# A decoder layer with routed experts: the last 48 rows of each expert's down weights split into high and low parts and stacked in 128 rows, and row numbers computed one block earlier

## The chip, the cores and the metric

The kernel runs on one core of one Trainium2 chip. The time is the device time of one execution in microseconds (us). The median of three runs of the kernel before is 344.32 us (343.75 to 344.35).

The engines in this text: PE is TensorE (matrix products), PEld its loading of stationary operands, DVE is VectorE, ACT is ScalarE, POOL is GpSimd, SP is SyncE, which here does nothing but wait, load registers and start DMAs.

## The reference

One decoder layer on 8 sequences of 128 rows of 256 values: self-attention with a sliding window, cross-attention, and a feed-forward part with 16 experts, of which each row takes four, plus a shared expert. The part that the change touches:

```
topk_w, topk_ids = top_k(softmax(x @ gate_w.T), 4)
for w13_e, w2_e, e in experts:            # 16 of them; w13_e is 352 x 256, w2_e is 256 x 176
    coef = sum(where(topk_ids == e, topk_w, 0))
    g, u = split(x @ w13_e.T)             # 176 and 176 columns
    acc += ((silu(g) * u) @ w2_e.T) * coef
out = shared(x) + acc
```

All inputs and outputs are float32.

## The kernel before

**Front (up to about 195 us).** Both attentions run as a software pipeline over the 8 sequences; `iteration(t)` is written out on each engine for the first and last values of t and is a loop for the middle ones. Beside it POOL splits the shared expert's weights (`split_shared`, a copy to the reduced type float32r and a subtraction that leaves the low part), and SP clears 17 MB of DRAM (`x_slots`). Routing follows: DVE computes the place of each of a row's four picks (`route_slots`), and POOL scatters the rows with 32 indirect DMAs (`scatter`, L538) into `x_slots`, where each expert's rows lie together. DVE and ACT split the experts' up weights into `w13_h` and `w13_l`; POOL does the last three low parts itself (L606).

**Block stage (about 195 to 314 us).** The rows of `x_slots` are worked off in 47 blocks of 128 rows, each for one expert. For a block n:

- SP loads the expert's down weights into `w2` (`load_down`, L432 and L433) and the block's rows into `xb` (`load_rows`, L424 to L426). Each takes a register load of the expert or row number from `table`, then a DMA. Both tiles have 4 buffers. `load_rows` waits until block n-4 has been transposed (`xbt_psum`) and its row numbers are made (`ids_ready`); `load_down` waits until the products of block n-4 are done (`yb_psum`). SP's order is `load_rows(n + 5)`, `load_down(n + 3)`, then the next n.
- PE transposes `xb` (`turn_block`, L1772), ACT copies it out as float32r (`take_rows_t`, L812), DVE subtracts for the low part (`low_rows_t`, L1270). PE makes the up product in six float32r matmuls (`block_up` through `three`, L1524: high by high, high by low, low by high, two halves each). ACT takes silu (`block_gate`, L820), DVE multiplies (`block_hidden`, L1278) into `hb`, padded from 176 to 256 columns with zeros. PE transposes it (`turn_hidden`, L1792), ACT copies it out (`take_hidden_t`, L827), and PE multiplies by `w2` in two float32 matmuls (`block_down`, L1802), each of which the trace shows as two records. DVE scales the result (`take_block`, L1285), and POOL writes it with an indirect DMA (`place_rows`, L613) to the places in `ids`, which DVE computes in three small steps (`block_ids`, L1290 to L1294).

PE's order in an iteration n is written out: `turn_block(n + 2)`, `block_up(n + 1)`, `turn_hidden(n)`, `block_down(n - 1)`. DVE's is `low_rows_t(n + 2)`, `block_hidden(n + 1)`, `block_ids(n + 1)`, `take_block(n - 1)`. ACT's is `take_rows_t(n + 2)`, `block_gate(n + 1)`, `take_hidden_t(n)`.

**End (314 us on).** PE finishes the second half of the shared expert, while SP gathers the experts' results into `yg`; DVE adds all up, and SP stores the output.

Of the kernel before, what the change touches and what calls it, by code (L numbers as in the profile page):

```python
# [7 lines left out]
F32 = mybir.dt.float32  # L8
F32R = mybir.dt.float32r
# [27 lines left out]
GU = 2 * HE  # L37
REGION = B * T
# [20 lines left out]
def decoder_layer(nc, x_in, ctx_in, keys_in, wqkv_in, bqkv_in, wo_in, bo_in, rope_in, masks_in, gate_in,  # L59
                  w13_in, w2_in, shared_in, ident_in, iota_in, tri_in, upto_in, table_in, picks_in, dump_in, packs_in, out):  # L60
    ctx = ExitStack()
    with ctx:
# [24 lines left out]
        ident_b = place("ident_b", [128, 128], BF16)  # L87
        masks = place("masks", [128, 2, TILES, 128], BF16)
        zero_b = place("zero_b", [128, 2 * XW], BF16)
# [91 lines left out]
        wo = place("wo", [128, KC, D])  # L181
        rope = place("rope", [128, 2, ROT])
# [4 lines left out]
        qkv = place("qkv", [128, QKV])  # L187
        turned = place("turned", [128, ROT])
# [32 lines left out]
        w2 = place("w2", [128, RB, KC, D])  # L221
        xbt_h = place("xbt_h", [128, 2, KC, 128], F32R)
        xbt_l = place("xbt_l", [128, 2, KC, 128], F32R)
        hb = place("hb", [128, 2, D])
        hbt = place("hbt", [128, 2, KC, 128])
        cursor[0] = max(cursor[0], after_cross)
        sb("slab", [128, (cursor[0] - base) // 4])
        x_slots = nc.dram_tensor("x_slots", [EMPTY + 128, XW], F32)
        y_picks = nc.dram_tensor("y_picks", [YROW, D], F32)
# [133 lines left out]
        hbt_ready = sem("hbt_ready")  # L363
        yb_psum = sem("yb_psum")
# [14 lines left out]
        def _(sp):  # L379
# [24 lines left out]
            for c in range(1, B):  # L404
                load_keys(c)
                if 2 <= c <= SC:
                    sp.wait_ge(swl_ready, c - 1)
                    sp.dma_start(sw_raw[:, :], shared_in[c - 1]).then_inc(sw_loaded, 16)
                if c == 1:
# [18 lines left out]
            def load_down(n):  # L428

                if n >= RB:  # L430
# [3 lines left out]
                             w2_in[bass.ds(e, 1)].rearrange("e p k d -> p (e k d)")).then_inc(w2_loaded[n % RB], 16)  # L434

            sp.wait_ge(x3_ready, B)
            sp.wait_ge(table_ready, 3)
            for n in range(RB - 1):
                load_down(n)
# [25 lines left out]
        def _(pool):  # L465
# [107 lines left out]
            for t in (B - 2, B - 1):  # L573
                iteration(t)
# [46 lines left out]
        def _(act):  # L621
# [193 lines left out]
            def block_gate(n):  # L815

                act.wait_ge(gu_psum, n + 1)
                if n >= 2:
                    act.wait_ge(hb_ready, n - 1)
                act.activation(sg[:, n % 2, :], ps_gu[n % 2][:, 0:HE], ACT.Silu).then_inc(sg_ready, 1)  # L820

            def take_hidden_t(n):

                act.wait_ge(hbt_psum, n + 1)
                if n >= 2:
                    act.wait_ge(yb_psum, n - 1)
                act.activation(hbt[:, n % 2, :, :], ps_ht[n % 2][:, 0:KC * 128].rearrange("p (k n) -> p k n", k=KC),  # L827
                               ACT.Copy).then_inc(hbt_ready, 1)
# [4 lines left out]
            for n in range(NBLK):  # L833
# [4 lines left out]
                take_hidden_t(n)  # L838

# [1079 lines left out]
```

## Time and profile before

| | us |
|---|---|
| median of three runs | 344.32 |
| the profiled execution | 343.41 |
| its span, first to last instruction | 341.6 |
| PE busy | 308.8 (90%) |
| DVE busy | 241.5 (71%) |
| ACT busy | 186.7 (55%) |
| POOL busy | 146.6 (43%) |

The profiled execution is one run; its span is 1.81 us shorter than its own time, and its own time is 0.91 us under the median. Times in the trace count from the start of the span. "Busy" is an average over stages with different limits; for a stage the waits and the queue of SP say more. In rows of the trace a merged row shows its start, its duration, the engine, the line, what is written from what, and how many instructions; the bracket at the end is the idle time before it and what ended it. SPq is SP's instruction queue; its DMA rows show when a DMA is issued, not when it lands.

### The profile page before, as it was taken

How to read it: one execution, taken by the hardware profiler on the slowest of the kernel's cores; microseconds unless marked ns; L12 is line 12 of the kernel's file. 1: busy time of each engine (PE TensorE's matmuls, PEld its weight loads, DVE VectorE, ACT ScalarE, POOL GpSimd, SP SyncE). 2: the span in 40 equal slices, each digit the busy share in tenths (PEclk: the TensorE clock that was granted, in tenths of full speed). 3: DMA queues.
4: the chain of work that ended last, by engine and by line, in shares of the span. 5: the costliest groups of instructions: out<-in, count | busy, mean ns of one | idle time of the engine just before them, and what ended most of it. 6: DMA issues, size and time to landing. Idle time of an engine off the chain costs nothing.

```text
span 341.6 us, 8504 instructions
## 1 busy us (share of the span) xinstructions
PE 308.8 (90%) x2606; PEld 238.2 (70%) x2608; DVE 241.5 (71%) x720; ACT 186.7 (55%) x538; POOL 146.6 (43%) x179
## 2 busy tenths in 40 slices
PE   6897899999999997879997789998999989999983
PEld 2354576667667764658775578787978979888862
DVE  2357788988888799563887856576766666765396
ACT  1052889888898977473697333343434434342231
POOL 3584133544544413487578253333434434345000
PEclk9999999999999998996999989999999999999998
DMA  7997197989899941023122526777777777774681
GB/s 210 302 389 307 25 310 179 302 248 291 242 264 266 239 141 33 16 98 113 54 94 96 157 66 187 214 218 233 209 230 210 220 224 213 229 220 149 249 319 61
DMA packets 44153, 66.84 MB, mean 196 GB/s; under 512 B 5347, under 2 KB 31988, under 8 KB 43604
## 3 DMA queue, kind: packets, MB, share of 16 engines
q1 hardware_dynamic: 39476, 54.91, 55.0%
q0 software_dynamic: 3792, 10.56, 8.1%
q10 hardware_dynamic: 848, 0.92, 1.2%
q8 instruction: 19, 0.31, 0.4%
q14 instruction: 18, 0.15, 0.2%
HBM read 37.07 MB, written 29.30 MB: 194 GB/s over the span
## 4 chain that ended last, share of the span: by engine, by line
PE 53%; DVE 9%; DMA 8%; issue 8%; SPq 8%; POOL 7%; ACT 6%; DVEq 0%; ACTq 0%; POOLq 0%
PE bank L1524 16%; PE bank L1802 6%; DMA xb<-x_slots 6%; POOL x_slots L538 5%; PE bank L1441 5%; PE bank L1450 5%; ACT probs L650 4%; PE bank L1394 3%; PE bank L1459 3%; SPq L425 3%; PE bank L1772 2%; SPq L432 2%; PE bank L1483 2%; PE bank L1792 2%; PE bank L1562 2%
## 5 line engine op out<-in xcount | busy, mean ns | idle before, releaser
L613 POOL DMA_INDIRECT y_picks<-yb,ids x47 | 45.1, 960 | 70.0 <-DVE yb L1285 69.4
L650 ACT ACTIVATE probs<-bank,neg_max 128x128 f32<-128x128 f32 x256 | 70.7, 399 | 2.7 <-DVE neg_max L903 2.5
L1802 PE MATMUL bank<-w,hbt 128*128 128x256 f32 x188 | 48.3, 380 | 0.0
L903 DVE TENSOR_REDUCE neg_max<-bank 128x4 f32<-128x512 f32 x64 | 42.1, 683 | 5.8 <-PE bank L1441 5.7
L1450 PE MATMUL bank<-ident,probs 128*128 128x128 f32 x256 | 36.9, 281 | 2.6 <-ACT probs L650 2.6
L812 ACT ACTIVATE xbt_h<-bank 128x256 fp32r<-128x256 f32 x47 | 18.0, 384 | 38.5 <-PE bank L1772 38.4
L538 POOL DMA_INDIRECT x_slots<-x,slots x32 | 34.5, 1080 | 9.3 <-issue 8.9
L1450 PEld LDWEIGHTS bank<-ident,probs 128*128 128x128 f32 x256 | 29.1, 143 | 12.4 <-ACT probs L650 10.3
L1802 PEld LDWEIGHTS bank<-w,hbt 128*128 128x128 f32 x188 | 32.1, 190 | 2.5
L1278 DVE TENSOR_TENSOR hb<-sg,bank 128x176 f32<-128x176 f32 x47 | 15.9, 337 | 24.0 <-ACT sg L820 24.0
L820 ACT ACTIVATE sg<-bank 128x176 f32<-128x176 f32 x47 | 14.9, 317 | 30.2 <-PE bank L1524 30.2
L1270 DVE TENSOR_TENSOR xbt_l<-bank,xbt_h 128x256 fp32r<-128x256 f32 x47 | 19.9, 424 | 11.6 <-ACT xbt_h L812 8.6
L1524 PE MATMUL bank<-w_h,xbt_h 128*128 x94 | 27.5, 373 | 0.0
L1772 PE MATMUL bank<-ident,xb 128*128 128x128 f32 x94 | 18.9, 284 | 6.8 <-DMA xb<-x_slots 6.5
L1285 DVE TENSOR_SCALAR yb<-bank,offset 128x256 f32<-128x256 f32 x47 | 22.7, 483 | 2.0 <-PE bank L1802 2.0
L1524 PE MATMUL bank<-w_h,xbt_l 128*128 x94 | 23.4, 331 | 0.0
L1524 PE MATMUL bank<-w_l,xbt_h 128*128 x94 | 23.3, 330 | 0.0
L1772 PEld LDWEIGHTS bank<-ident,xb 128*128 128x128 f32 x94 | 12.0, 143 | 15.2 <-DMA xb<-x_slots 9.2
L509 POOL TENSOR_TENSOR rstd<-ve,expo 128x1 f32<-128x1 f32 x16 | 9.1, 570 | 26.0 <-DVE ve L953 26.0
L485 POOL TENSOR_TENSOR turned<-qkv,rope 128x320 f32<-128x320 f32 x8 | 6.9, 863 | 29.5 <-DVE qkv L884 29.5
L827 ACT ACTIVATE hbt<-bank 128x256 f32<-128x256 f32 x47 | 18.0, 383 | 1.8 <-PE bank L1792 1.8
L1792 PE MATMUL bank<-ident,hb 128*128 128x128 f32 x94 | 18.0, 273 | 0.7 <-issue 0.5
(175 smaller groups left out, 677.6 us busy)
## 6 DMA issues: line engine op xcount, KB each, us to landing
x_slots<-zero_b SPq DMA_DIRECT2D x16, 1072.0 KB, 10.9
w<-w_in_dram SPq DMA_DIRECT2D x47, 256.0 KB, 3.1
xb<-x_slots SPq DMA_DIRECT2D x47, 134.0 KB
w<-w_in_dram SPq DMA_DIRECT2D x4, 1408.0 KB, 12.6
yg<-y_picks SPq DMA_DIRECT2D x8, 512.0 KB, 7.0
sw_raw<-shared_in_dram SPq DMA_DIRECT2D x6, 384.0 KB, 3.4
ktc<-keys_in_dram SPq DMA_DIRECT2D x8, 256.0 KB, 3.2
ctx_sb<-ctx_in_dram SPq DMA_DIRECT2D x1, 1024.0 KB, 12.6
```

Source lines behind the costliest of these rows:

```text
L538: pool.indirect_dma_start(x_slots[:, :], bass.IndirectOffsetOnAxis(slots[:, TOPK * b + k:TOPK * b + k + 1], 0), x[:, b, :], None).then_inc ...
L613: pool.indirect_dma_start(y_picks[:, :], bass.IndirectOffsetOnAxis(ids[:, n:n + 1], 0), yb[:, n % RB, :], None).then_inc(yb_placed[n % RB] ...
L650: ins = act.activation(probs[:, g, j, :], ps_s[kind][g][:, 128 * j:128 * j + 128], ACT.Exp, bias=neg_max[:, kind, g, j:j + 1])
L812: act.activation(xbt_h[:, n % 2, :, :], ps_xt[n % 2][:, 0:KC * 128].rearrange("p (k n) -> p k n", k=KC), ACT.Copy).then_inc(xbt_high, 1)
L903: dve.tensor_reduce(neg_max[:, kind, g, :], ps_s[kind][g].rearrange("p (j n) -> p j n", j=BLK), AX.X, ALU.max, negate=True).then_inc(max_r ...
L1270: dve.tensor_tensor(xbt_l[:, n % 2, :, :], ps_xt[n % 2][:, 0:KC * 128].rearrange("p (k n) -> p k n", k=KC), xbt_h[:, n % 2, :, :].bitcast( ...
L1285: dve.tensor_scalar(yb[:, n % RB, :], ps_yb[n % 2][:, 0:D], offset[:, n % RB, 1:2], None, ALU.mult).then_inc(yb_ready, 1)
L1450: ins = pe.transpose(ps_s[kind][g][:, 128 * j:128 * j + 128], probs[:, g, j, :], ident[:, :])
L1524: ins = pe.matmul(outs, w, m, start=first and i == 0, stop=last and i == len(todo) - 1, skip_group_check=not (first and last))
L1772: ins = pe.transpose(ps_xt[n % 2][:, 128 * k:128 * k + 128], xb[:, n % RB, 128 * k:128 * k + 128], ident[:, :])
L1792: ins = pe.transpose(ps_ht[n % 2][:, 128 * k:128 * k + 128], hb[:, n % 2, 128 * k:128 * k + 128], ident[:, :])
L1802: ins = pe.matmul(ps_yb[n % 2][:, 0:D], hbt[:, n % 2, k, :], w2[:, n % RB, k, :], start=k == 0, stop=k == KC - 1)
```

## The change

**Down weights.** An expert's down weights have 176 rows. Before, they stand in DRAM as 256 rows with 80 of zeros. Now the first 128 rows stay float32 (`w2_in`), and the last 48 come as an input of their own (`tail_in`, padded to 64 rows). In the front, SP loads them into `tail`, POOL makes a float32r high part `tail_h` (after its `iteration(B - 2)`) and the remainder `tail_l` (after its `iteration(B - 1)`), 8 x 256 values in each of 128 partitions, in two halves each. SP copies the first 128 rows from DRAM to DRAM into a new tensor `w2_split` (2 MB) and stores both parts there with four DMAs (2 MB in all). So the second 128 rows of an expert are 64 high and 64 low ones. `load_down` reads `w2_split`, as many bytes as before. DVE waits for the stores (`tail_stored`) before `gated(0)`, which writes where `tail_h` lies; SP waits for them and for the copy before the first `load_down`.

**Products.** `block_hidden` becomes two instructions: columns 0 to 127, and the last 48 written twice, at 128 and at 192. ACT's `take_hidden_t` becomes two: the transposed second half as float32r (`hbt_h`), the first as float32. DVE gets a new `low_hidden_t`, the remainder `hbt_l` of the second half. `block_down` becomes one float32 matmul and two float32r ones with the same stacked 128 rows, one with `hbt_h` and one with `hbt_l`; the last waits for `low_hidden_t`.

**Moves.** `take_block` goes from DVE to ACT (after `take_hidden_t(n)`). `block_ids` runs one block earlier: in an iteration n it makes the numbers of block n + 2, and those of blocks 0 and 1 come ahead of `block_hidden(0)`.

PE at the end of one block iteration and the start of the next, before (`w_148` is `w2`, `w_h` and `w_l` are the up weights' parts):

```order
L1524 MATMUL bank<-w_h,xbt_l 128x352 x2
L1758 REGISTER_ALU
L1759 REGISTER_ALU
L1792 MATMUL bank<-ident,hb 128x128 x2
L1802 MATMUL bank<-w_148,hbt 128x256 x2
L1772 MATMUL bank<-ident,xb 128x128 x2
```

and now (`w_149` is `w2`):

```order
L1592 MATMUL bank<-w_h,xbt_l 128x352 x2
L1826 REGISTER_ALU
L1827 REGISTER_ALU
L1860 MATMUL bank<-ident,hb 128x128 x2
L1870 MATMUL bank<-w_149,hbt 128x256
L1871 MATMUL bank<-w_149,hbt_h 128x256
L1873 MATMUL bank<-w_149,hbt_l 128x256
L1840 MATMUL bank<-ident,xb 128x128 x2
```

One of the two float32 products has given way to two float32r ones; nothing else on PE has moved.

DVE at the start of the block stage, before:

```order
L1270 TENSOR_TENSOR xbt_l<-bank,xbt_h 128x256 x2
L1278 TENSOR_TENSOR hb<-sg,bank 128x176
L1290 SCALAR_TENSOR_TENSOR found<-xb,of_block 128x8
L1293 TENSOR_REDUCE offset<-found 128x2
L1294 SCALAR_TENSOR_TENSOR ids<-offset,dump 128x1
L1270 TENSOR_TENSOR xbt_l<-bank,xbt_h 128x256
L1278 TENSOR_TENSOR hb<-sg,bank 128x176
L1290 SCALAR_TENSOR_TENSOR found<-xb,of_block 128x8
```

and now:

```order
L1334 TENSOR_TENSOR xbt_l<-bank,xbt_h 128x256 x2
L1359 SCALAR_TENSOR_TENSOR found<-xb,of_block 128x8
L1362 TENSOR_REDUCE offset<-found 128x2
L1363 SCALAR_TENSOR_TENSOR ids<-offset,dump 128x1
L1359 SCALAR_TENSOR_TENSOR found<-xb,of_block 128x8
L1362 TENSOR_REDUCE offset<-found 128x2
L1363 SCALAR_TENSOR_TENSOR ids<-offset,dump 128x1
L1342 TENSOR_TENSOR hb<-sg,bank 128x128
L1345 TENSOR_TENSOR hb<-sg,bank 128x2x48
L1334 TENSOR_TENSOR xbt_l<-bank,xbt_h 128x256
```

The row numbers of blocks 0 and 1 have moved ahead of the first `hb`, which is two instructions.

POOL between its last two front iterations and the first scatter, now (the row at L564 is the subtraction of `split_shared`, L526 before):

```order
L622 CAST tail_h<-tail 128x1024 x2
L547 TENSOR_TENSOR rstd_73<-ve_72,expo 128x1 x2
L571 COPY x<-xn_82 128x256
L554 COPY c_pad<-ctx_sb 128x16x16
L562 CAST sw_h<-sw_raw 128x768
L564 TENSOR_TENSOR sw_l<-sw_raw,sw_h 128x768
L614 TENSOR_TENSOR tail_l<-tail,tail_h 128x1024 x2
L547 TENSOR_TENSOR rstd_73<-ve_72,expo 128x1
L576 DMA x_slots<-x,slots 16512x268
```

The rows at L622 and L614 are new; before, the same sequence ran without them.

The diff, cut:

```
+            sp.dma_start(w2_split[:, :, 0, :], w2_in).then_inc(w2_copied, 16)
             sp.wait_ge(swl_ready, SC)
...
+            for i, part, done in ((0, tail_h, tail_high), (1, tail_l, tail_low)):
+                sp.wait_ge(done, 2)
+                for half in range(2):
+                    es = slice(NE // 2 * half, NE // 2 * half + NE // 2)
+                    sp.dma_start(w2_split[es, TAIL * i:TAIL * i + TAIL, 1, :].rearrange("e r d -> r e d"),
+                                 part[TAIL * half:TAIL * half + TAIL, :, :].bitcast(F32)).then_inc(tail_stored, 16)
...
+            iteration(B - 2)
+            pool.wait_ge(tail_loaded, 16)
+            pool.wait_ge(v_ready, B)
+            for i in range(2):
+                es = slice(NE // 4 * i, NE // 4 * i + NE // 4)
+                pool.tensor_copy(tail_h[:, es, :], tail[:, es, :]).then_inc(tail_high, 1)
+            iteration(B - 1)
+            pool.wait_ge(tail_high, 2)
+            split_tail(0)
+            split_tail(1)
             inverse_deviation(CROSS, B - 3)
...
+            dve.wait_ge(tail_stored, 64)
             gated(0)
...
-                pe.wait_ge(hbt_ready, n + 1)
+                pe.wait_ge(hbt_copied, 2 * n + 2)
...
-                for k in range(KC):
-                    ins = pe.matmul(ps_yb[n % 2][:, 0:D], hbt[:, n % 2, k, :], w2[:, n % RB, k, :], start=k == 0, stop=k == KC - 1)
-                ins.then_inc(yb_psum, 1)
+                outs, w_tail = ps_yb[n % 2][:, 0:D], w2[:, n % RB, 1, :].bitcast(F32R)
+                pe.matmul(outs, hbt[:, n % 2, :], w2[:, n % RB, 0, :], start=True, stop=False, skip_group_check=True)
+                pe.matmul(outs, hbt_h[:, n % 2, :], w_tail, start=False, stop=False, skip_group_check=True)
+                pe.wait_ge(hbt_ready, n + 1)
+                pe.matmul(outs, hbt_l[:, n % 2, :], w_tail, start=False, stop=True, skip_group_check=True).then_inc(yb_psum, 1)
...
+            def low_hidden_t(n):
+                dve.wait_ge(hbt_copied, 2 * n + 2)
+                dve.tensor_tensor(hbt_l[:, n % 2, :], ps_ht[n % 2][:, 128:256], hbt_h[:, n % 2, :].bitcast(F32), ALU.subtract
+                                  ).then_inc(hbt_ready, 1)
...
-                if n + 1 < NBLK:
-                    block_ids(n + 1)
-                if n >= 1:
-                    take_block(n - 1)
-            take_block(NBLK - 1)
+                if n + 2 < NBLK:
+                    block_ids(n + 2)
+                low_hidden_t(n)
```

## Rows read from the trace of the kernel before

**Rows 1.** Busy time, 254 to 294 us: PE, PEld, DVE, ACT, POOL, clock, DMA, GB/s.

```profile
254.00:294.00 40.00, 38.98 (x237) 34.94 (x236) 27.46 (x102) 16.90 (x51) 15.83 (x17) 1.00 0.75 218
```

**Rows 2.** The chain that ended last: start, duration, engine, line, count.

```profile
231.13 4.30 DMA xb<-x_slots
...
305.64 0.96 PE bank L1524 x6
306.82 0.86 PE bank L1802 x4
307.91 0.96 PE bank L1524 x6
...
313.96 16.81 PE bank L1524 x72
```

**Rows 3.** DMAs in SP's queue: start of the issue, its duration.

```profile
202.47 0.34 SPq L426 DMA_DIRECT2D xb<-x_slots  x1
209.33 0.34 SPq L426 DMA_DIRECT2D xb<-x_slots  x1
226.59 0.34 SPq L426 DMA_DIRECT2D xb<-x_slots  x1
228.86 0.34 SPq L426 DMA_DIRECT2D xb<-x_slots  x1
304.12 0.34 SPq L426 DMA_DIRECT2D xb<-x_slots  x1
```

**Rows 4.** SP's waits: two rows for 190 to 315 us, one for 200 to 207.

```profile
SPq L424 <- DVE ids L1294: 6.4, 6, 3.0
SPq L432 <- PE bank L1802: 1.4, 2, 1.0
...
SPq L424 <- DVE ids L1294: 3.9, 2, 3.0
```

**Rows 5.** All engines at the start of the block stage, in order of time.

```profile
196.31 4.94 POOL L606 TENSOR_TENSOR w_l<-w,w_h 128x704 fp32r<-128x704 f32 x3 [5.64 <-DVE hid_l L1179]
...
199.18 0.42 DVE L1270 TENSOR_TENSOR xbt_l<-bank,xbt_h 128x256 fp32r<-128x256 f32 x1 [1.08 <-ACT xbt_h L812]
...
200.97 0.31 DVE L1290 SCALAR_TENSOR_TENSOR found<-xb,of_block 128x8 f32<-128x8 f32 x1
```

**Rows 6.** The page's groups of the block stage: busy, mean ns of one.

```profile
L1278 DVE TENSOR_TENSOR hb<-sg,bank 128x176 f32<-128x176 f32 x47 | 15.9, 337 | 24.0 <-ACT sg L820 24.0
...
L827 ACT ACTIVATE hbt<-bank 128x256 f32<-128x256 f32 x47 | 18.0, 383 | 1.8 <-PE bank L1792 1.8
```

**Rows 7.** POOL and DVE, in order of time, at two places of the front.

```profile
10.47 0.87 POOL L485 TENSOR_TENSOR turned<-qkv,rope 128x320 f32<-128x320 f32 x1 [3.67 <-DVE qkv L884]
10.53 0.85 DVE L897 COPY v_pad<-qkv 128x64 f32<-128x64 f32 x1
...
120.31 0.18 DVE L897 COPY v_pad<-qkv 128x64 f32<-128x64 f32 x1
```

**Rows 8.** POOL's last shared-weight subtraction and its next instruction.

```profile
132.82 1.81 POOL L526 TENSOR_TENSOR sw_l<-sw_raw,sw_h 128x768 fp32r<-128x768 f32 x1
139.94 0.55 POOL L509 TENSOR_TENSOR rstd<-ve,expo 128x1 f32<-128x1 f32 x1 [5.31 <-DVE ve L953]
```

**Rows 9.** DVE from 135 to 164 us, in order of time.

```profile
135.02 0.16 DVE L1028 COPY x<-top_f 128x16 f32<-128x16 f32 x1
...
136.12 0.17 DVE L1032 SCALAR_TENSOR_TENSOR slots<-top_f,slot_s 128x16 uint32<-128x16 f32 x1
136.22 0.68 DVE L915 COPY values_t<-bank 128x512 f32<-128x512 f32 x1
137.79 0.69 DVE L909 COPY probs_tc<-bank 128x512 f32<-128x512 f32 x1 [0.90 <-PE bank L1450]
...
138.68 0.42 DVE L929 TENSOR_TENSOR attn<-bank,inv 128x256 f32<-128x256 f32 x1
...
163.29 0.69 DVE L1174 TENSOR_TENSOR hid<-silu,bank 128x512 f32<-128x512 f32 x1
```

More of the change, by code:

```diff
@@ L37 @@
 GU = 2 * HE
+TAIL = 64
 REGION = B * T
@@ L363, in decoder_layer @@
         hbt_ready = sem("hbt_ready")
+        hbt_copied = sem("hbt_copied")
+        tail_loaded = sem("tail_loaded")
+        tail_high = sem("tail_high")
+        tail_low = sem("tail_low")
+        tail_stored = sem("tail_stored")
+        w2_copied = sem("w2_copied")
         yb_psum = sem("yb_psum")
@@ L408, in _ @@
                     sp.dma_start(sw_raw[:, :], shared_in[c - 1]).then_inc(sw_loaded, 16)
+                if c == 5:
+                    sp.dma_start(tail[:, :, :], tail_in).then_inc(tail_loaded, 16)
                 if c == 1:
@@ L572, in _, with split_tail @@
                 iteration(t)
-            for t in (B - 2, B - 1):
-                iteration(t)
+            def split_tail(i):
+                es = slice(NE // 4 * i, NE // 4 * i + NE // 4)
+                pool.tensor_tensor(tail_l[:, es, :], tail[:, es, :], tail_h[:, es, :].bitcast(F32), ALU.subtract
+                                   ).then_inc(tail_low, 1)
+            iteration(B - 2)
+            pool.wait_ge(tail_loaded, 16)
+            pool.wait_ge(v_ready, B)
+            for i in range(2):
+                es = slice(NE // 4 * i, NE // 4 * i + NE // 4)
+                pool.tensor_copy(tail_h[:, es, :], tail[:, es, :]).then_inc(tail_high, 1)
[3 more added lines that the diff above has]
+            split_tail(1)
             inverse_deviation(CROSS, B - 3)
@@ L826, in take_hidden_t, with take_block @@
                     act.wait_ge(yb_psum, n - 1)
-                act.activation(hbt[:, n % 2, :, :], ps_ht[n % 2][:, 0:KC * 128].rearrange("p (k n) -> p k n", k=KC),
-                               ACT.Copy).then_inc(hbt_ready, 1)
+                act.activation(hbt_h[:, n % 2, :], ps_ht[n % 2][:, 128:256], ACT.Copy).then_inc(hbt_copied, 1)
+                act.activation(hbt[:, n % 2, :], ps_ht[n % 2][:, 0:128], ACT.Copy).then_inc(hbt_copied, 1)
+            def take_block(n):
+                act.wait_ge(yb_psum, n + 1)
+                act.wait_ge(ids_ready, n + 1)
+                if n >= RB:
+                    act.wait_ge(yb_placed[n % RB], 16 * (n // RB))
+                act.activation(yb[:, n % RB, :], ps_yb[n % 2][:, 0:D], ACT.Copy, scale=offset[:, n % RB, 1:2]).then_inc(yb_ready, 1)
             take_rows_t(0)
@@ L838, in _ @@
                 take_hidden_t(n)
+                if n >= 1:
+                    take_block(n - 1)
+            take_block(NBLK - 1)
             for n in range(SC + AHEAD, 2 * SC):
@@ L1786, in turn_hidden @@
             def turn_hidden(n):
-                pe.wait_ge(hb_ready, n + 1)
+                pe.wait_ge(hb_ready, 2 * n + 2)
                 if n >= 2:
                     pe.wait_ge(hbt_ready, n - 1)
-                for k in range(KC):
+                for k in range(2):
                     ins = pe.transpose(ps_ht[n % 2][:, 128 * k:128 * k + 128], hb[:, n % 2, 128 * k:128 * k + 128], ident[:, :])
```

62 lines of the change are left out of this document (42 added, 20 removed).

## The prediction

> **What bounds the kernel now.** I read the table of busy time by stretch first. In the block stage PE is busy 38.98 of 40 us, DVE 27.46, ACT 16.90, POOL 15.83, with the clock at its upper level [rows 1]. That says PE, but the chain of waits says less: it runs in turns through PE alone, one block every 2.27 us (305.64 to 307.91) [rows 2], and through stretches in which SP issues one DMA after another until a row load that lands 4.30 us later releases PE [rows 2]. So I read SP's queue next. At its fastest SP also needs 2.27 us for a block (226.59 to 228.86), that is 1.135 us for each of its two loads, of which the issue itself is 0.34 [rows 3]. PE and SP are equally fast at their best, and neither holds it: from the row load at 209.33 (block 7) to the one at 304.12 (block 46) lie 39 blocks and 94.79 us, 2.43 us for a block [rows 3]. What slows SP is in its waits: 6.4 us for the row numbers, 1.4 for PE's products; 3.9 of the 6.4 lie at the start, before 207 us [rows 4]. After the last row load PE still needs until 313.96 [rows 2], 9.84 us; from there 16.81 us of the shared expert are PE's alone [rows 2], and the end follows.
>
> Ahead of the block stage the chain runs through PE, ACT and DVE to POOL's scatters; a delay of DVE there moves everything behind it.
>
> **Part by part.** *The products.* The four records of L1802 take 0.86 us, 0.215 each for 256 columns [rows 2]. A float32r matmul takes 0.96 / 6 = 0.160 us for 352 columns and, in the last stretch, 16.81 / 72 = 0.233 for 512 [rows 2]; the line through both gives 0.116 for 256 (an estimate, with 0.160 as its upper bound and 0.107, the 352-column figure reduced by a third, as its lower). The new `block_down` is 2 x 0.215 + 2 x 0.116 = 0.66, so PE's block falls from 2.27 to about 2.07 us (2.05 to 2.16). This is worth 0.2 us a block only where PE sets the pace, and SP's 2.27 is next.
>
> *Row numbers earlier.* `load_rows(n)` needs the numbers of block n - 4. They were made after the hidden values of the block that follows it; now a block sooner, some 2 us more room. The steps cost the same. I count the later waits of SP as gone. Then the pace is SP's own: 2.27 at its best; the mean of the 39 blocks without the waits that are listed after 207 us is (94.79 - 2.5 - 1.4) / 39 = 2.33. I take 2.31, nearer to the second because slow issues stay.
>
> *The start.* SP's fifth row load came at 202.47, after the numbers of block 0 [rows 3]. These now come straight after the second low part, which ends at 199.60 [rows 5]. But POOL works on three subtractions from 196.31 to 201.25, the third from about 199.6, and the step at 200.97 took 0.31 and ended at 201.28, just behind POOL [rows 5]. I take it that it now waits for the same end: the fifth load stays at 202.47, and five loads of 1.135 later block 7's goes out at 208.15 instead of 209.33. (If DVE gets in first, 1.3 us more; if the later waits return at once, nothing.) `block_hidden(0)` is about 1.6 us later, queued behind both sets of numbers on DVE, and PE waits for it; PE's shorter blocks recover that by block 7.
>
> So block 46's rows are asked for at 208.15 + 39 x 2.31 = 298.2, 5.9 us earlier. Behind it, four `block_down`s are shorter by 0.8 together; at the last block PE waits some 0.3 for the two ACT copies and DVE's remainder: 0.5 gained. The block stage is worth **6.4 us**.
>
> *DVE and ACT in a block.* DVE loses one 256-column step and gains one of 128 and the second instruction of `hb`: at most 0.42 (half of which is the likelier) and 0.337 [rows 5, 6] against a step removed that is as long as the first. A block costs DVE at most 0.34 us more; 27.46 of 40 us becomes at most 33 [rows 1], which SP's pace covers. ACT gets the result (as large as L827, 0.383) and one more copy of at most 0.383 [rows 6]: over 16 blocks at most 12.3 us on 16.90 [rows 1], covered too. `take_block` waits on ACT for a write begun four blocks earlier; behind it are only copies that PE needs a block later.
>
> *POOL in the front.* Two casts and two subtractions of 1,024 columns. 768 columns take 1.81 us in a subtraction [rows 8], so 2.41 each. The casts fall in an idle time and cost nothing. The subtractions begin at 134.63, where POOL is idle until 139.94 [rows 8], and end at about 139.5: POOL itself loses nothing. But DVE does. At 10.53 a copy on DVE that else takes 0.18 took 0.85 and ended at 11.38, as POOL's instruction from 10.47 to 11.34 did [rows 7]: it waited for POOL to end. DVE's copy at 135.02 [rows 9] now meets the first subtraction and waits until about 137.1; the two steps between put `slots` (L1032), with both inputs in SBUF like the step at 200.97 [rows 5], at 138.2, where it meets the second and waits until 139.5. Then `values_t` comes at 139.6 instead of 136.22. Some of it is covered: DVE waited 0.90 for PE before 137.79 [rows 9]. So `attn`, at 138.68 [rows 9], follows the new end of `values_t` (140.3) by PE's turn and the reciprocal, at 141.2: **2.5 us** later, on the chain. Bounds: 0, if neither waits or only `slots` waits for the first subtraction (it then lasts until 137.1, within the 0.90); 1.2 if the copy alone waits; 3.4 if nothing covers it.
>
> The Trainium skill (SBUF — State Buffer, section SBUF: two separate sides) says that VectorE, with two SBUF inputs or in a two-port mode, and GpSimd share one port pair, which whoever starts first holds for its whole instruction. By that both steps wait, the 2.5; by the copy's row alone it would be 1.2. No row before shows L1032 itself beside a POOL subtraction.
>
> *DMAs in the front.* SP now queues 1 MB of `tail`, the 2 MB copy and 2 MB of stores before the table is needed. The block stage's last front DMAs leave room: DVE's new wait stands before L1174, at 163.29 [rows 9], with `route_slots`, the low parts and so POOL's later scatters queued behind it. The stores of the low parts go out at about 140, so they have 23 us. I cost this at nothing.
>
> **The sum.** 6.4 - 2.5 = 3.9 us: 343.41 becomes 339.5 in the profiled execution, its span 337.7. That execution is 0.91 under the median; against 344.32 it is **340.4 us**.
>
> **Rivals.** *No meeting on the port* (0.27): DVE's steps get through, the front costs 0 to 1.2; the time is 337.9 (1.0 less if the start gains too). For it: both steps are very short, and only a longer copy and one late step are seen waiting. Against: rows 7.
>
> *VectorE sets the pace* (0.08, slower): `low_hidden_t` stands last in DVE's block and waits for two ACT copies, and the next low part and row numbers wait behind it, so that SP waits again. It decides where DVE's round exceeds 2.43 us. At 2.43 only the start (1.2) and the end (0.5) are gained against 2.5 lost: 345.1; each 0.05 us above costs 2 us more. For it: two steps more in a block and a wait between engines. Against: DVE's share [rows 1] and a third of it idle.
>
> *Late stores* (0.03, slower): each us that they land after 165.8 (163.29 plus the 2.5) delays the scatters by a us; from about 170 on the kernel is slower.
>
> *The float32r products are no cheaper* (0.06; the change then does not do what it says): PE stays at 2.27, SP at 2.31, and the two stand in each other's way a little: perhaps 2.36 for a block (2 us more) and no gain at the end (0.5 more), 342.9.
>
> The forecast itself has 0.48; 0.05 is left for a pace between, at which gain and cost cancel, and 0.03 for a gain beyond these.
>
> **How the numbers follow.** About 0.2% (0.7 us) is what a measurement of this kernel can tell from no change. The range: downwards to the case without the port and with the early start, 336.5; upwards the pace of 2.36 instead of 2.31 (2 us) and the 0.9 that nothing covers, 343.0. Faster gets the forecast, the port rival, the case of products no cheaper and the gain beyond: 0.84. Slower 0.11, the same 0.05.
>
> **What would show it.** Right: row loads in SP's queue every 2.27 to 2.35 us, with hardly a wait for `ids`; the records of `block_down` at 0.66 us a block; PE idle 0.2 us a block until a row load lands; `attn` of the last sequence some 2.5 us later, with `slots` and the copy before it stretched to POOL's ends. Wrong: SP waiting for DVE or PE again, a float32r matmul of 256 columns above 0.16 us, or `attn` at its old time.

## The result, and the profile after

The changed kernel is slower. Its median is 347.21 us (four executions, 345.98 to 349.43) against 344.03 for the kernel before in the same comparison; the ratio is 1.014, with a 95% interval of 1.009 to 1.019. Some executions of a kernel run in a slower state; the ratio is estimated without them, and the quotient of the two medians is 1.009, the lower end of its interval. The forecast was 340.4, in a range of 336.5 to 343.0. The profiled execution took 345.98 us, with a span of 344.1, 2.5 longer than the 341.6 before.

Three marks of the trace tell where the difference lies. The first is the first row load that SP issues. Before (durations in a merged row cover several issues):

```profile
194.58 10.31 SPq L426 DMA_DIRECT2D xb<-x_slots  x6
```

SP's queue after, row loads only (start of the issue, its duration), where [rows 3] stands for before:

```profile
199.29 8.79 SPq L462 DMA_DIRECT2D xb<-x_slots  x6
...
212.47 0.34 SPq L462 DMA_DIRECT2D xb<-x_slots  x1
...
226.64 0.34 SPq L462 DMA_DIRECT2D xb<-x_slots  x1
...
228.91 0.34 SPq L462 DMA_DIRECT2D xb<-x_slots  x1
...
249.90 1.24 SPq L462 DMA_DIRECT2D xb<-x_slots  x1
...
307.02 0.34 SPq L462 DMA_DIRECT2D xb<-x_slots  x1
```

The row load at 212.47 is that of block 7, the one at 307.02 that of block 46. The blocks' end is in the chain that ended last, where PE's last products and the first of the last stretch stand:

```profile
314.96 0.43 PE bank L1870 x2
315.40 0.12 PE bank L1871
315.51 0.12 PE bank L1873
...
316.43 16.88 PE bank L1592 x72
```

So the profiled executions compare with the prediction's terms as follows.

| part | before | after | difference | forecast |
|---|---|---|---|---|
| front, to the first row load | 194.58 | 199.29 | +4.7 | +2.5 |
| first row load to that of block 7 | 14.75 | 13.18 | -1.6 | -1.2 |
| 39 blocks, to the row load of block 46 | 94.79 | 94.55 | -0.2 | -4.7 |
| from there to the end of the blocks | 9.84 | 9.41 | -0.4 | -0.5 |
| sum | | | +2.5 | -3.9 |

Two terms are right and two are wrong: the front costs 2.2 us more than forecast, and the pace of the blocks gains 4.5 less.

**The pace.** A round of SP at its best is still 2.27 us (226.64 to 228.91), and the mean of the 39 blocks is 94.55 / 39 = 2.424, where it was 2.431. PE is less busy in the same stretch as [rows 1] (PE, PEld, DVE, ACT, POOL, clock, DMA share, GB/s):

```profile
254.00:294.00 40.00, 36.78 (x238) 34.10 (x237) 25.72 (x119) 24.48 (x84) 15.47 (x17) 1.00 0.76 220
```

38.98 of 40 us have become 36.78: PE is faster, and waits. Its waits from 200 to 320 us (total, times, longest) and below them SP's from 207 to 320, as [rows 4]:

```profile
PE bank L1840 <- DMA xb<-x_slots: 11.3, 12, 2.9
```

```profile
SPq L468 <- PE bank L1873: 2.0, 5, 1.0
SPq L461 <- PE bank L1840: 1.2, 5, 0.3
```

The waits for row numbers are gone from there on, as forecast. But SP waits for PE 3.2 us instead of 1.8, and some issues are long (1.24 us at 249.90 instead of 0.34): what its issues take beyond 0.34 us adds up to 1.8 us over the 39 blocks, 0.8 before. PE in turn waits 11.3 us for the rows that SP asks for, 2.7 before.

**The front.** POOL's subtractions, and DVE beside them (start, duration), where [rows 9] stands for before:

```profile
135.89 4.66 POOL L614 TENSOR_TENSOR tail_l<-tail,tail_h 128x1024 fp32r<-128x1024 f32 x2
```

```profile
136.32 1.96 DVE L1091 COPY x<-top_f 128x16 f32<-128x16 f32 x1
...
139.23 1.35 DVE L1095 SCALAR_TENSOR_TENSOR slots<-top_f,slot_s 128x16 uint32<-128x16 f32 x1
...
142.41 0.42 DVE L992 TENSOR_TENSOR attn<-bank,inv 128x256 f32<-128x256 f32 x1
```

The copy took 1.96 us instead of 0.16 and ended at 138.28, as the first subtraction did (135.89 and half of 4.66 make 138.22); `slots` took 1.35 instead of 0.17 and ended at 140.58, as the second did (140.55). `attn` came at 142.41 instead of 138.68. But 1.3 us of this were there before the subtractions began. The chain shows what they are: two stretches in which PE waits for nothing that the profile shows, inside one group of products and behind another, that the trace of before doesn't have. (L1509 and L1566 belong to the attention; "issue" is such a wait.)

```profile
122.24 1.09 PE bank L1509 x28
123.33 1.17 issue
124.50 0.49 PE bank L1509 x3
...
125.83 0.13 PE bank L1566
125.97 1.09 issue
```

After `attn` another us is lost on the way to the first row load: the mean granted clock from 160 to 180 us is 0.86 of full speed in the trace of after and 0.97 in that of before.

### The profile page after: what moved, and what is told of

It reads as the page before. It is cut to its first block, busy times and chain, and to the rows that moved or that the text cites. A ratio compares the mean times of both kernels' runs of the same rounds, so it can differ in the third digit from the quotient of the medians.

```text
span 344.1 us, 8663 instructions
## 1 busy us (share of the span) xinstructions
PE 302.7 (88%) x2608; PEld 236.4 (69%) x2608; DVE 241.2 (70%) x767; ACT 208.8 (61%) x632; POOL 154.2 (45%) x183
## 4 chain that ended last, share of the span: by engine, by line
PE 48%; DMA 12%; SPq 9%; DVE 9%; issue 9%; POOL 7%; ACT 6%; DVEq 0%; ACTq 0%; POOLq 0%
PE bank L1592 14%; DMA xb<-x_slots 9%; POOL x_slots L576 5%; PE bank L1509 5%; PE bank L1518 5%; ACT probs L702 4%; PE bank L1462 3%; SPq L461 3%; PE bank L1870 2%; PE bank L1551 2%; SPq L468 2%; PE bank L1840 2%; PE bank L1527 2%; SPq L462 2%; SPq L469 2%
## 5 line engine op out<-in xcount | busy, mean ns | idle before, releaser
L576 POOL DMA_INDIRECT x_slots<-x,slots x32 | 35.5, 1108 | 9.3 <-issue 8.9
L1840 PE MATMUL bank<-ident,xb 128*128 128x128 f32 x94 | 19.3, 287 | 11.5 <-DMA xb<-x_slots 11.3
L888 ACT ACTIVATE yb<-bank,offset 128x256 f32<-128x256 f32 x47 | 22.3, 474 | 10.7 <-PE bank L1873 10.6
L1870 PE MATMUL bank<-w,hbt 128*128 128x256 f32 x94 | 28.2, 382 | 0.0
L1342 DVE TENSOR_TENSOR hb<-sg,bank 128x128 f32<-128x128 f32 x47 | 13.5, 288 | 18.6 <-ACT sg L872 18.6
L1871 PE MATMUL bank<-w,hbt_h 128*128 128x256 f32 x47 | 22.1, 470 | 0.0
L1840 PEld LDWEIGHTS bank<-ident,xb 128*128 128x128 f32 x94 | 10.8, 142 | 15.5 <-DMA xb<-x_slots 12.0
L709 ACT ACTIVATE probs_tc<-bank 128x512 f32<-128x512 f32 x24 | 15.0, 625 | 7.0 <-PE bank L1518 6.6
## 6 DMA issues: line engine op xcount, KB each, us to landing
xb<-x_slots SPq DMA_DIRECT2D x47, 134.0 KB, 3.0
```

Of the source, the lines that this page charges most:

```text
L576: pool.indirect_dma_start(x_slots[:, :], bass.IndirectOffsetOnAxis(slots[:, TOPK * b + k:TOPK * b + k + 1], 0), x[:, b, :], None).then_inc ...
L888: act.activation(yb[:, n % RB, :], ps_yb[n % 2][:, 0:D], ACT.Copy, scale=offset[:, n % RB, 1:2]).then_inc(yb_ready, 1)
L1840: ins = pe.transpose(ps_xt[n % 2][:, 128 * k:128 * k + 128], xb[:, n % RB, 128 * k:128 * k + 128], ident[:, :])
L1870: pe.matmul(outs, hbt[:, n % 2, :], w2[:, n % RB, 0, :], start=True, stop=False, skip_group_check=True)
L1871: pe.matmul(outs, hbt_h[:, n % 2, :], w_tail, start=False, stop=False, skip_group_check=True)
```

## Experiments

All experiments ran beside the kernel before. A kernel's executions spread over some 2 to 8 us, and the median of the kernel before was between 341.95 and 342.93 us there, about 1 to 2 us under that of the first comparison, so ratios are what is to be compared. The pace in the table is that of the 39 blocks in the one profiled execution; `attn` is that of the last sequence. Five of the kernels have one and the same block stage (changed, block_copy, no_sub, small_sub, early_sub), and their paces lie between 2.376 and 2.435: a difference in pace of 0.06, 2.3 us over the 39 blocks, can be that of two executions.

| kernel | median, us | ratio to before (95%) | `attn` | pace |
|---|---|---|---|---|
| before | 344.03 | 1 | 138.68 | 2.431 |
| changed | 347.21 | 1.014 (1.009 to 1.019) | 142.41 | 2.424 |
| ids_only | 340.62 | 0.995 (0.992 to 0.998) | 138.02 | 2.371 |
| front_only | 348.22 | 1.018 (1.016 to 1.021) | 143.14 | 2.418 |
| block_copy | 341.11 | 0.999 (0.995 to 1.003) | 140.32 | 2.378 |
| no_sub | 340.90 | 0.995 (0.993 to 0.998) | 137.94 | 2.435 |
| small_sub | 340.52 | 0.996 (0.992 to 1.000) | 138.32 | 2.376 |
| early_sub | 341.97 | 0.997 (0.993 to 1.001) | 139.64 | 2.430 |
| after_static | 333.68 | 0.975 (0.969 to 0.982) | 143.08 | 2.070 |
| before_static | 337.81 | 0.984 (0.977 to 0.990) | 137.97 | 2.316 |
| best | 329.41 | 0.963 (0.956 to 0.969) | 138.43 | 2.116 |
| before_words | 341.78 | 0.997 (0.993 to 1.000) | 137.95 | 2.379 |
| ids_back | 347.79 | 1.012 (1.006 to 1.017) | 143.10 | 2.532 |
| words_ids | 337.14 | 0.988 (0.981 to 0.996) | 139.62 | 2.254 |

My theory after reading the trace of the changed kernel was: SP's round, two register loads and two DMAs, holds the pace whether VectorE or PE is faster; and POOL's two subtractions are most of the front's cost. The rivals: DMA landing or DMA load holds the pace; the DMAs that the front got are its cost.

### The parts of the change by themselves

**ids_only**, the kernel before with the row numbers ahead:

```
-            block_hidden(0)
             block_ids(0)
+            block_ids(1)
+            block_hidden(0)
...
-                if n + 1 < NBLK:
-                    block_ids(n + 1)
+                if n + 2 < NBLK:
+                    block_ids(n + 2)
```

> The kernel before with one part of the change: the row numbers of a block made a block further ahead on VectorE. By the prediction's sum (waits for the row numbers are what keeps SP's queue above its floor) the start gains 1.2 us and the pace falls from 2.43 to at most 2.33 us a block, since PE's block is still 2.27: 39 x 0.10 + 1.2 = 5 us, about 339 us. By the theory formed on the trace of the changed kernel (SP's queue keeps 2.42 us a block without those waits: its slow issues and PE's products end last instead) at most the start is left: 343 to 344.5 us, pace 2.40 to 2.44 us.

It lies between both: 1.6 us under the kernel before, with a pace of 2.371. From 207 us on SP no longer waits for row numbers, but for PE:

```profile
SPq L425 <- PE bank L1773: 1.9, 8, 0.3
SPq L432 <- PE bank L1803: 1.5, 2, 0.8
```

That is 3.4 us of waits where before had 4.3 (2.5 for the row numbers, 1.8 for PE). Removing the wait that the profile named has let another one show. The pace is 0.06 lower, half of the forecast gain, but no more than two executions of one block stage can differ by; what is shown is the time, 0.5%.

**front_only**, the new front with the block stage of before (against the changed kernel; the lines that make the blocks' products and moves those of before again are left out here):

```
-            sp.dma_start(w2_split[:, :, 0, :], w2_in).then_inc(w2_copied, 16)
+            sp.dma_start(w2_split[:, :, 0, :], first_in).then_inc(w2_copied, 16)
...
-                             w2_split[bass.ds(e, 1)].rearrange("e p k d -> p (e k d)")).then_inc(w2_loaded[n % RB], 16)
+                             w2_in[bass.ds(e, 1)].rearrange("e p k d -> p (e k d)")).then_inc(w2_loaded[n % RB], 16)
```

> The changed kernel's front (load of the last rows, casts and subtractions on GpSimd, copy and stores to the split weights, VectorE's and SP's waits for the stores) with the block stage of the kernel before, which reads its padded weights and not the split ones. The prediction put the front at 2.5 us: 344.0 + 2.5 = 346.5 us, attn of the last sequence 2.5 us later. By the trace of the changed kernel it is 4.7 us until the first row load: 348.7 us, with 1.3 of it before the subtractions begin and 0.7 to 0.9 behind attn at a lower clock.

The front costs 1.8%, 6 us, more than the forecast and than the trace of the changed kernel had said. What the whole block stage gives back is the rest up to the changed kernel's 1.4%: 0.4%, some 1.5 us (the intervals allow from nothing to 3.3), not 6.4.

**block_copy**, the new block stage without the front's new work except one copy:

```
-            sp.dma_start(w2_split[:, :, 0, :], w2_in).then_inc(w2_copied, 16)
+            sp.dma_start(w2_split[:, :, :, :], w2_in).then_inc(w2_copied, 16)
...
-            pool.wait_ge(tail_high, 2)
-            split_tail(0)
-            split_tail(1)
```

> The changed kernel's block stage; its front without the load of the last rows, casts, subtractions and stores: one copy on SP's queue, of 4 MB, makes the weights that the blocks read, so the low part of the split is left out of the output. Prediction: no cost in the front, 6.4 us gained in the blocks, 337.6 us, pace 2.31. By the trace of the changed kernel (2.2 us gained in the blocks, pace 2.42): 341.8 us, or up to 343.1 us where the copies' DMAs and not GpSimd are behind PE's stalls of 1.3 us at 122 to 127 us.

No more than 0.5% of gain lies in the interval. With front_only this says the same from the other side: the new block stage is worth hardly anything, though in it PE's block is shorter.

**ids_back**, the changed kernel with the row numbers where they were:

```
-                if n + 2 < NBLK:
-                    block_ids(n + 2)
+                if n + 1 < NBLK:
+                    block_ids(n + 1)
```

> The changed kernel with the row numbers made where the kernel before made them (all work is kept): the split products alone, with the front. If the products bring nothing while SP sets the pace, and the row numbers brought the 1.6 us that the kernel before gained from them alone, this is 1.6 us slower than the changed kernel: about 348 to 349 us. If the products alone bring what I forecast and the row numbers nothing: 347 us. If row numbers a block later now hold SP again, since VectorE has more to do in a block: 351 us or more.

Inconclusive by time: its interval and that of the changed kernel overlap. In its trace SP waits again for the row numbers, 5.7 us in 7 waits from 207 us on, and the pace is 2.532; this profiled execution was the longest of its five.

### What costs the front

**no_sub**, the changed kernel without the two subtractions, all else kept (the second store writes the high parts again):

```
-            for i, part, done in ((0, tail_h, tail_high), (1, tail_l, tail_low)):
+            for i, part, done in ((0, tail_h, tail_high), (1, tail_h, tail_high)):
...
-            split_tail(0)
-            split_tail(1)
```

> The changed kernel without GpSimd's two subtractions (the store of the low parts writes the high parts a second time, so the low part of the split is left out of the output); casts, load, copy and stores stay. If only the port that the subtractions hold delays VectorE, as predicted, 2.5 us of 347.2 go: 344.7 us, and attn comes 2.5 us sooner than in the changed kernel. If the lower clock after it is the same delay's doing (PE idle while it waits for VectorE), 3.2 us go: 344.0 us. The stalls of 1.3 us at 122 to 127 us stay by either. If DMAs are behind all of it, nothing changes: 347 us.

It falls by more than either theory said: from 1.014 to 0.995, which is 6.4 us (the intervals allow 4.6 to 8.3; the medians, each against that of before beside it, give 4.5). So the tail's load, the copy, the stores and the casts cost nothing that shows, and the two subtractions all. In the trace the copy and `slots` have their old times, and `attn` comes 4.5 us sooner than in the changed kernel:

```profile
135.02 0.16 DVE L1082 COPY x<-top_f 128x16 f32<-128x16 f32 x1
...
136.13 0.17 DVE L1086 SCALAR_TENSOR_TENSOR slots<-top_f,slot_s 128x16 uint32<-128x16 f32 x1
...
137.94 0.42 DVE L983 TENSOR_TENSOR attn<-bank,inv 128x256 f32<-128x256 f32 x1
```

**small_sub**, the same subtractions in eight pieces at the same place:

```
-                es = slice(NE // 4 * i, NE // 4 * i + NE // 4)
+                es = slice(NE // 16 * i, NE // 16 * i + NE // 16)
...
-            split_tail(0)
-            split_tail(1)
+            for i in range(8):
+                split_tail(i)
```

> The changed kernel with GpSimd's two subtractions of 1,024 columns cut into eight of 256 at the same place (all work is kept). If a subtraction holds VectorE's copy and slots until its own end, as read from the changed kernel's trace (1.96 and 1.35 us where 0.16 and 0.17 are normal), each now waits at most 0.6 us: of the 4.1 us by which attn stands later than without the subtractions, about 2.5 to 3 come back, and the time falls from 347 to about 344 us. If the whole run of subtractions is what delays VectorE, or something else in them, nothing comes back: 347 us.

All of it comes back, 0.996, with all of the work in place; 2.5 to 3 us were expected. POOL takes 0.86 us more for the eight (5.52), and DVE's two steps get in between:

```profile
134.54 5.52 POOL L614 TENSOR_TENSOR tail_l<-tail,tail_h 128x256 fp32r<-128x256 f32 x8
```

```profile
134.96 0.34 DVE L1091 COPY x<-top_f 128x16 f32<-128x16 f32 x1
...
136.24 0.43 DVE L1095 SCALAR_TENSOR_TENSOR slots<-top_f,slot_s 128x16 uint32<-128x16 f32 x1
...
138.32 0.42 DVE L992 TENSOR_TENSOR attn<-bank,inv 128x256 f32<-128x256 f32 x1
```

The copy took 0.34 and `slots` 0.43, so each waited for what was left of one piece. The cost was the length of one instruction, not the work.

**early_sub**, eight pieces in POOL's idle time at 124 and 130 us:

```
+            inverse_deviation(CROSS, B - 4)
+            pool.wait_ge(tail_high, 2)
+            for i in range(4):
+                split_tail(i)
+            inverse_deviation(SELF, B - 2)
+            keep_rows(B - 4)
+            pad_context(B - 2)
+            for i in range(4, 8):
+                split_tail(i)
+            split_shared(B - 3)
```

> The changed kernel with the subtractions in eight pieces of 256 columns, four behind the inverse deviation at 123 us and four behind the copy of the context at 129 us, where GpSimd is idle 3.7 and 2.7 us and VectorE has neither the copy nor slots (all work is kept). If the meeting with these two steps is the front's whole cost, the time is that of the changed kernel without subtractions: 341 to 342 us against 342 before. If GpSimd's work costs VectorE wherever it stands, it stays at 344 to 347 us.

342.0 us, as the first theory expects. In eight pieces the place made no difference that these runs can tell.

### What sets the pace

**after_static** and **before_static**: SP's load of the down weights with a fixed expert, without the register load, in the changed kernel and in the kernel before:

```
-                e = sp.value_load(table[0:1, n:n + 1], min_val=0, max_val=NE - 1)
+                e = n % NE
```

> The changed kernel with a fixed expert (block number modulo 16) in SP's load of the down weights in place of the number loaded into a register: the weights are of the same size, but the choice of the expert is left out, so the output is another one. If SP's round of two register loads and two DMAs (2.27 us at its best) sets the pace, it gets shorter and PE's 2.07 us a block comes next: up to 39 x 0.35 = 13 us less than the changed kernel, 334 to 339 us. If the landing of the row loads or another engine sets it, the pace stays at 2.4 and the time at 347 us.

> The kernel before with the same fixed expert in SP's load of the down weights (the choice of the expert is left out of the output). PE's block of 2.27 us is as long as SP's round at its best, so a shorter SP round gives back only what lies above it: 39 x 0.15 = 6 us at most, 336 to 338 us, and less where VectorE's row numbers are late as before. If SP's queue is not what sets the pace: 342 us as the kernel before.

Both fall as the theory of SP's round expects, the changed kernel by 3.9 of a hundred (just below the range expected) and the kernel before by 1.6. In the changed kernel SP's best round is now 1.62 us, 0.65 less (row loads only):

```profile
209.39 0.33 SPq L462 DMA_DIRECT2D xb<-x_slots  x1
...
211.01 0.33 SPq L462 DMA_DIRECT2D xb<-x_slots  x1
...
212.63 0.33 SPq L462 DMA_DIRECT2D xb<-x_slots  x1
```

The 0.65 are not the load alone. `value_load` is three kinds of instruction in the changed kernel's trace, the load, a step on registers and an assertion on the value (ns: least, median, most):

```profile
L468 SPq TENSOR_LOAD <-table x47: 263/269/731, 191.0 to 310.6; - x47
L468 SPq FUSED_REGOPS  x47: 152/152/183, 191.7 to 310.9; - x47
L468 SPq SEQ_ASSERT  x47: 18/18/32, 192.0 to 311.1; - x47
```

Two short steps that form the address follow. In a round at the best pace it is 0.71 us from the start of the load (227.03) to the issue (227.74). The fixed expert takes all of this out, so these runs don't show what the load by itself would give back.

and PE never waits: in the 40 us from 240 on (columns as above) it is busy all the time, and blocks follow each other as the prediction had it, 2.08 us each (the chain that ended last):

```profile
240.00:280.00 40.00, 40.00 (x273) 38.62 (x271) 29.68 (x136) 27.23 (x97) 18.37 (x20) 1.00 0.85 257
```

```profile
242.79 0.97 PE bank L1592 x6
243.98 0.43 PE bank L1870 x2
244.87 0.97 PE bank L1592 x6
```

The rival falls: the DMA engines moved more than in the changed kernel (257 GB/s against 220) and delivered in time. In before_static the pace is 2.316, just above PE's 2.27, and SP waits for the row numbers 22.8 us from 207 us on, in 38 waits: with a shorter round the row numbers are what SP meets next.

**words_ids** and **before_words**: a register load avoided with the computation kept. PE already reads the expert numbers six to a word; SP now does the same, in the kernel before with and without the earlier row numbers:

```
-                e = sp.value_load(table[0:1, n:n + 1], min_val=0, max_val=NE - 1)
+                r = turns[n % 2]
+                sp.reg_alu(r, packed_sp[n // PACK], 4 * (n % PACK), ALU.logical_shift_right)
+                sp.reg_alu(r, r, NE - 1, ALU.bitwise_and)
+                e = sp.snap(r, min_val=0, max_val=NE - 1)
```

> All work is kept: the kernel before with SP's expert numbers from the packed words, nothing else. SP's round falls below PE's 2.27 us, and as with the fixed expert the row numbers, made late, are waited for instead (28 us in 41 waits there): 337 to 339 us against 342 to 343 before. If the register load is not what costs in SP's round: 342 us.

> All work is kept: the kernel before with the row numbers a block further ahead and SP's expert numbers from the packed words; no split products and nothing new in the front. With SP's round at 1.86 us and the row numbers in time, PE's 2.27 us a block is left as the pace: 39 x 0.10 to 0.15 us less than the row numbers alone (340.6 us), 335 to 337 us. Against the kernel with everything and the same relief for SP (329.4 us) this tells what the split products are worth once SP doesn't hold them: 39 x 0.19 = 7.4 us by the records, less the front's cost. If PE's own pace was not what came next, it is 340 us.

before_words misses its expectation: 341.8 instead of 337 to 339. Its SP waits 15.5 us for the row numbers in 30 waits, 4.6 of them before 207 us, which was expected, but its pace is 2.379, not the 2.316 of before_static; why the two differ is not settled. With the row numbers ahead (words_ids) the time is 337.1, at the upper end of what was expected, and PE is busy 40.00 of 40 us from 240 on, at 2.27 us a block.

**best**, everything together: the changed kernel with eight pieces and with SP's numbers from the words:

```
-                es = slice(NE // 4 * i, NE // 4 * i + NE // 4)
+                es = slice(NE // 16 * i, NE // 16 * i + NE // 16)
...
-                e = sp.value_load(table[0:1, n:n + 1], min_val=0, max_val=NE - 1)
...
+                e = sp.snap(r, min_val=0, max_val=NE - 1)
```

> All work is kept: the changed kernel with the subtractions in eight pieces, and with SP's expert numbers taken from the packed words that PE already reads, one register load in six blocks and a shift and a mask for each block in place of a register load. By the theory that SP's round sets the pace (a fixed expert in its place gave 2.08 us a block, and a round of 1.62 at its best) the round is about 1.62 + two register instructions + a sixth of 0.65, some 1.9 to 2.0 us, and PE's 2.08 sets the pace: 39 x 0.3 = 12 us less than the kernel with eight pieces, 327 to 331 us. If shift and mask cost what the load costs, nothing: 340 us.

329.4 us, 3.7% under the kernel before (0.956 to 0.969), as expected. SP's round is 1.86 us at its best (row loads only), and PE is busy throughout from 240 to 280 us:

```profile
204.95 0.34 SPq L462 DMA_DIRECT2D xb<-x_slots  x1
...
206.81 0.34 SPq L462 DMA_DIRECT2D xb<-x_slots  x1
...
208.67 0.34 SPq L462 DMA_DIRECT2D xb<-x_slots  x1
```

```profile
240.00:280.00 40.00, 40.00 (x268) 38.16 (x267) 29.18 (x134) 27.07 (x95) 18.20 (x20) 1.00 0.85 255
```

Four kernels, all with the row numbers ahead and without the cost of the long subtractions, put the split products' worth in one table (ratio to before):

| | SP loads each number | SP takes it from words |
|---|---|---|
| float32 products (ids_only, words_ids) | 0.995 | 0.988 |
| split products (small_sub, best) | 0.996 | 0.963 |

While SP holds the pace the split products are worth nothing that shows (0.995 and 0.996, each within 0.3 to 0.4 of a hundred); once it doesn't, 0.963 / 0.988, or 2.6% (1.6 to 3.6 by the intervals). The second row has the rest of the new front and the moves to ACT in it, so this is what the change is worth with them.

## Why the prediction was wrong, step by step

Two terms of the sum failed: the pace of the blocks (-4.7 forecast, -0.2 measured) and the size of the front's cost (+2.5 forecast, +4.7 in the profiled execution and some 6 by the runs).

**The products** were right. The chain shows 0.43 + 0.12 + 0.12 = 0.67 us for a `block_down`, 0.66 forecast; PE's block was to be 2.07 and is 2.08 in after_static, where nothing holds it.

**The row numbers and the pace** are the step that failed first. I counted the waits for the row numbers as gone, subtracted them from the mean and got 2.33 us a block, then took 2.31. The waits did go. But a mean less its waits isn't the pace: the queue is then ahead by that much, and meets what was hidden behind the wait, here PE's products. Of 4.3 us of waits before, 3.2 stand in the changed kernel, for PE, and the longer DMA issues (1.8 us beyond the usual instead of 0.8) took the rest. These issues differ from one execution to the next: small_sub, with the same block stage, had 0.5 us of them and 92.69 us for the 39 blocks instead of 94.55; but even that is a gain of only 2.1 where 4.7 was forecast. This term was -4.7 and measured -0.2 in the trace of the changed kernel; in ids_only, where the pace is 2.371, it would be -2.3. I had named SP's 2.27 as next behind PE's, rightly, and still gave most of the gain to a pace at that floor. A loop in which two partners wait for each other, with floors of 2.27 for SP and 2.07 to 2.27 for PE, runs at 2.37 to 2.44 in the six kernels with unrelieved SP and the numbers ahead. The term that would have mattered is the register load with its check and address, 0.65 us of SP's round, which I had as a part of the 1.135 and did not take apart. The Trainium skill (DMA: Bandwidth & Descriptors, section Latency and other measured facts) gives some 600 ns as the floor of a `tensor_load`; the trace does not agree: here the load's own record has a median of 0.27 us, and the rest of the 0.65 lies behind it.

**The start and the end** were right: -1.6 against -1.2, and -0.4 against -0.5. The start came by the way that was forecast: the last step of block 0's row numbers took 1.41 us and ended at 205.76, as POOL's third low part did (205.75).

**The port** was right as a mechanism. Both steps waited, as forecast, and the runs with eight pieces and without subtractions show that the subtractions are the cause. The Trainium skill (SBUF — State Buffer, section SBUF: two separate sides) says that the port pair is held for a whole instruction; 1.96 and 1.35 us beside subtractions of 2.33, and 0.34 and 0.43 beside pieces of 0.69, agree. The rival without a meeting falls.

**Its size** failed: 2.5 us forecast, 6.4 by the ratios of the changed kernel and no_sub, 5.4 by their first row loads. The parts that the traces show: DVE's `attn` lies 4.5 us later than without subtractions. Of this 1.3 are there before the subtractions begin, and 3.2 come from the two steps; the 0.90 wait for PE [rows 9] that I had counted as cover is only 0.15 in no_sub. It belonged to that one execution: from 134.0 to 137.5 us its granted clock was 0.51, nearly all at the lower level of 1.2 GHz, and 1.00 in no_sub. That `attn`, less the 1.3, stands at 141.1 where 141.2 was forecast is therefore in part luck. Then 0.9 follow until the first row load; from 160 to 180 us the mean granted clock is 0.86 against 1.00.

The runs show that this lower clock goes with the long subtractions, a term that the forecast put at nothing. While DVE is held, PE stands idle. Here are 134 to 141 us in the changed kernel and in no_sub (columns as in [rows 1]):

```profile
134.00:141.00 7.00, 2.35 (x20) 1.21 (x20) 6.90 (x10) 4.61 (x17) 6.47 (x4) 1.00 1.06 317
```

```profile
134.00:141.00 7.00, 5.63 (x54) 3.75 (x58) 5.18 (x16) 4.88 (x15) 2.03 (x3) 1.00 1.06 334
```

PE is busy 2.35 to 2.90 us of these 7 in the four kernels with the long subtractions (changed, front_only, after_static, ids_back) and 4.23 to 6.29 in the ten others; from 137 to 147 us the mean granted clock is then 0.83, 0.66, 0.51 and 0.51 in the four, and 1.00 in the others, but for 0.98 in before and 0.89 in block_copy. Over the whole span, on average over all executions on record, the four kernels have 0.962 to 0.968 and the others 0.973 or more. The difference, about 0.012 of 345 us, is 4 us of PE at full speed, an estimate of the most that it can cost. How much of the 6.4 it is no run separates, since no run holds DVE without PE standing idle.

**Open** are the 1.3 us at 122 to 127 us. They can't be the work of subtractions that start at 135.89. In after_static, ids_back, front_only, block_copy and words_ids 1.6 to 1.8 us are lost near that place as well (the cross attention's rows come at 132.5 to 132.7 instead of 130.9), two of these without any subtraction of the change. There the clock accounts for the loss in size: each of the five has some 3.4 us at the lower level, beginning between 118.6 and 120.1 us, and half of that is 1.7. In the changed kernel the clock is 1.00 there and PE stands still in "issue". The four traces with the long subtractions all have a loss there, of the ten others three have one (the third is early_sub, at a clock of 1.00). A profile of one execution for each kernel can't tell chance from a cause here, and no run tests it.

**The DMAs in the front** cost nothing, as forecast: no_sub has all of them. **VectorE's pace, late stores and products no cheaper** all fall: DVE is busy 25.72 of 40 us, its wait for the stores does not show, the products are at 0.67. The kernel became slower by none of the paths that I had priced as slower, but by an expected cost that was larger and a gain that another queue kept.

Two bounds of the stated range don't follow from its terms: 340.4 and 2 and 0.9 make 343.3, not 343.0, and 337.9 less the 1.0 to 1.3 of an early start makes 336.6 to 336.9, not 336.5. Nothing else hangs on these.

## What to carry to other kernels

Before a gain on one engine is booked, look at the floor of every queue in the same loop, the DMA-issuing one too, and ask what its round consists of: here a faster PE was worth nothing that showed until the 0.65 us of a register load, its check and its address left SP's round, and then 2.6%. A wait taken out of a loop's mean is an upper bound of the gain, since the next wait takes its place. Long GpSimd instructions beside short VectorE steps on the critical path are best cut into pieces: eight instead of two cost GpSimd 0.9 us and gave the kernel some 6 (4 to 8 by the intervals).

## What the runs showed of the hardware

- A VectorE step of 0.16 us lasted 1.96 beside a GpSimd subtraction of 1,024 columns and ended with it; beside pieces of 256 columns (0.69 us) the same two steps took 0.34 and 0.43 us, at most 0.26 more than alone.
- On SP a register load (0.27 us by its record), its check and its address cost about 0.65 us of a round (2.27 to 1.62); a shift and a mask in their place, with the address, cost about 0.24 (1.62 to 1.86).
- DMA issues on SP, 0.34 us as a rule, last 0.4 to 1.4 us now and then. Two executions of the same block stage had 1.8 and 0.5 us of this in the 39 blocks, and took 94.55 and 92.69 us for them.
- PE's granted clock, with its two levels of 1.2 and 2.4 GHz, is at the lower one for some 3.4 us, from 118.6 to 120.1 us on, in five of the fourteen traces, of kernels with and without the change, though PE was busy 5.8 of the 6 us before. From 137 to 147 us it is 0.51 to 0.83 in the four kernels in which PE had stood idle for over 4 of 7 us.
